# Decoder block with latent attention: the five constant products among the first 22 score chunks are taken out

## The reference, cut to what matters

```python
def mla_attention(x, Wq, Wdkv, Wuk, Wuv, Wo, ln_g, ln_b):
    q = (x @ Wq.T).reshape(b, t, N_HEADS, HEAD_DIM).transpose(0, 2, 1, 3)      # 16 heads of 16
    latent = layernorm(x @ Wdkv.T, ln_g, ln_b)
    k = (latent @ Wuk.T)...; v = (latent @ Wuv.T)...
    q = apply_rope(q); k = apply_rope(k)
    scores = jnp.einsum('bhqd,bhkd->bhqk', q, k) / np.sqrt(HEAD_DIM)
    scores = jnp.where(causal, scores, -jnp.inf)
    attn = jax.nn.softmax(scores, axis=-1)
    out = jnp.einsum('bhqk,bhkd->bhqd', attn, v)...
    return out @ Wo.T
```

## Time and profile before

| what | value |
|---|---|
| median of three runs | 2792.73 us |
| profiled execution | 2797.18 us, span 2795.4 us |
| TensorE busy | 2654.7 us, 95% of the span |
| VectorE, ScalarE, GpSimd busy | 50%, 39%, 11% |
| mean granted TensorE clock | 0.984 |
| DMA | 20 GB/s over the span |

### The profile page before, as it was taken

The page is one execution under the profiler, slowest core; times in us unless marked ns, Lnnn a source line. Parts: engine busy times, 40 slices in busy tenths (PEclk is TensorE's granted clock), DMA queues, the critical chain, the costliest instruction groups (busy, mean ns, idle before and its releaser), DMA issues.

```text
span 2795.4 us, 43692 instructions
## 1 busy us (share of the span) xinstructions
PE 2654.7 (95%) x16702; PEld 1644.3 (59%) x16703; DVE 1395.2 (50%) x3906; ACT 1089.9 (39%) x2028; POOL 299.3 (11%) x457
## 2 busy tenths in 40 slices
PE   7999999999999999999999999999999999978998
PEld 4555655455565664455556564455556564448997
DVE  3334356754334456754333467753343567753443
ACT  3444233543444224444443333434443424431221
POOL 2000010112000010212000010212000010222111
PEclk9999999999999999999999999999999999988999
DMA  3000000001000000001000000001000000032111
GB/s 99 12 12 1 16 1 1 2 14 42 12 12 0 16 1 1 2 14 42 17 7 1 16 1 1 2 14 48 12 6 1 16 1 2 1 149 78 54 56 36
DMA packets 32426, 57.11 MB, mean 20 GB/s; under 512 B 6980, under 2 KB 23442, under 8 KB 31858
## 3 DMA queue, kind: packets, MB, share of 16 engines
q1 hardware_dynamic: 27490, 41.56, 4.7%
q0 software_dynamic: 4752, 13.02, 1.3%
HBM read 40.24 MB, written 14.32 MB: 20 GB/s over the span
## 4 chain that ended last, share of the span: by engine, by line
PE 89%; ACT 4%; DVE 3%; issue 2%; POOL 2%; DMA 0%; SPq 0%; DVEq 0%; ACTq 0%; POOLq 0%
PE ps L959 10%; PE ps L1176 9%; PE ps L931 8%; PE ps L904 8%; PE ps L1210 7%; PE ps L1228 6%; PE ps L889 5%; PE ps L949 5%; PE ps L1303 5%; PE ps L1317 4%; PE ps L914 4%; PE ps L1051 3%; PE ps L1069 2%; PE ps L844 2%; PE ps L860 2%
## 5 line engine op out<-in xcount | busy, mean ns | idle before, releaser
L1405 DVE TENSOR_REDUCE neg_max<-ps 128x1 f32<-128x128 f32 (+7 forms) x256 | 194.1, 758 | 565.6 <-PE ps L934 565.3
L1176 PE MATMUL ps<-arena 32*128 32x512 f32 (+3 forms) x1536 | 446.3, 529 | 11.0 <-DVE arena L1592 6.5
L797 ACT ACTIVATE arena<-ps 128x1024 f32<-128x1024 f32 (+1 forms) x320 | 300.1, 939 | 367.6 <-PE ps L1210 367.5
L1210 PE MATMUL ps<-arena 32*128 32x256 f32 (+1 forms) x2560 | 364.6, 388 | 0.0
L959 PE MATMUL ps<-arena 128*128 128x512 f32 (+3 forms) x768 | 319.6, 503 | 4.7 <-ACT arena L715 0.5
L715 ACT ACTIVATE arena<-ps 128x512 f32<-128x512 f32 (+3 forms) x384 | 188.3, 491 | 296.5 <-PE ps L949 294.4
L931 PE MATMUL ps<-arena 128*128 128x512 f32 (+3 forms) x768 | 290.7, 489 | 4.4 <-ACT arena L724 4.4
L1210 PEld LDWEIGHTS ps<-arena 32*128 32x128 f32 x2560 | 210.5, 183 | 116.3 <-issue 99.3
L904 PE MATMUL ps<-turned_t,arena 128*128 128x512 f32 x512 | 227.8, 598 | 1.1 <-ACT turned_t L686 1.1
L931 PEld LDWEIGHTS ps<-arena 128*128 128x128 f32 x768 | 139.0, 190 | 135.4 <-issue 114.8
L949 PE MATMUL ps<-ident,arena 128*128 128x128 f32 x1152 | 193.1, 278 | 20.8 <-ACT arena L703 11.4
(11 more groups left out here) (215 smaller groups left out, 3852.7 us busy)
## 6 DMA issues: line engine op xcount, KB each, us to landing
arena<-in_w_qkv SPq DMA_DIRECT2D x32, 384.0 KB, 3.1
arena<-in_w SPq DMA_DIRECT2D x2, 4096.0 KB, 16.7
xin<-in_x SPq DMA_DIRECT2D x5, 1024.0 KB, 5.5
xres_ids<-sorted_res SPq DMA_DIRECT2D x35, 129.0 KB, 2.2
xin<-sorted_rows SPq DMA_DIRECT2D x35, 128.0 KB, 2.1
w_out<-in_w_out SPq DMA_DIRECT2D x1, 1024.0 KB
out<-xin,out_row POOLq DMA_INDIRECT x35, 2.8
sorted_res<-xin SPq DMA_DIRECT2D x4, 129.0 KB, 2.5
```

The lines of the kernel that those rows point to most:

```text
L797: nc.scalar.activation(mprobs_t[n % BUFS][:, 2 * pair:2 * pair + 2, 0:QUARTER + more], ps[:, bank:bank + 2, 0:QUARTER + more], ACT.Exp).th ...
L1176: last = nc.tensor.matmul(ps[:, MAX_BANK[m], at:at + n], q_heads_t[rows_j, g, t * P:(t + 1) * P], k_heads_t[rows_j, g, c * BANK:c * BANK + ...
L1210: last = nc.tensor.matmul(ps[:, 3 + j, kb * QUARTER:kb * QUARTER + n_q], k_heads_t[rows_j, g, keys_at:keys_at + P], q_heads_t[rows_j, g, ( ...
L1405: nc.vector.tensor_reduce(neg_max[:, par, t:t + 1], ps[:, buf:buf + 2, :].rearrange("p a n -> p (a n)")[:, 0:n], AX.X, ALU.max, negate=Tru ...
```

## The change

The loop over chunks 6 to 21 with its five calls of `keep_warm` is replaced by one call of `chunks`, which issues the same chunks in the same order. Nothing else is touched: the calls of `keep_warm` at other places stay.

```diff
                 for use in range(NG, 2 * NG):
                     turn_keys(use)
                 pe.wait_ge(kt_taken, b * (2 * NG) + 2 * NG)
-                for s in range(6, ISSUED):
-                    chunks(s, s + 1)
-                    if s % 3 == 2:
-                        keep_warm(1, 7)
+                chunks(6, ISSUED)
                 pe.wait_ge(ms_taken, b * MAX_SLOTS + WIDE)
```

## The result

The changed kernel takes 2819.64 us (median of four runs, 2815.16 to 2820.55) against 2792.72 us before: the ratio of the means is 1.0089, with a 95% interval of 1.0072 to 1.0107. It is slower, by 27 us in the medians, where 11 us were forecast; 2819.64 us also lies above the forecast's own range of 2796 to 2818 us. The profiled execution of it took 2815.16 us with a span of 2813.4 us, 18.0 us more than the profiled execution before. It is the fastest of the four runs, so the profile shows less loss than the median has.

The account below looks back on a forecast made before the run. TensorE, busy for 95% of the span, was taken as the bound. Per batch, 4.7 us lost in items less 1.9 us gained gives +2.8; 2792.7 + 4 x 2.8 = 2803.9, stated as 2804 us (own range 2796 to 2818; 8 in 10: 2788 to 2820).

Parts of the forecast that it names:

- The clock falls in all four batches: Chunks 6 to 21: without constant products, 32-row chunks are too little work, so the clock falls to 0.50 about midway.
- The items: Items after the chunks: 14 us of low clock at 1.5 times the time, 4.7 us lost per batch.
- The chunks: Chunks 6 to 21: low clock costs the last five chunks 1.6 us, leaving 1.9 of 3.5 us gained per batch.
- The sum against the profiled execution: Whole kernel: batches two to four +8.4 us, first batch -1.1, from the profiled 2797.2 us to 2804.5 us.
- The high-clock schedule: Chunk 6 to the items, clock high: chunks 7 to 10 side by side, then VectorE paces; items 3.5 us earlier per batch.
- hold (2779 us): Rival, chunks 6 to 21: the clock holds, each batch keeps its 3.5 us, 2779 us; chance 0.10.
- come back as the items begin (2790 us): Rival, start of items: they restore the fallen clock at once, -0.7 us per batch, 2790 us; chance 0.18.
- stay low through the stage: Rival, items: the clock stays low for a whole stage, 54 to 77 us per batch, 2850 us and above; chance 0.05.

Follow-up runs that it names:

- e1_thin: Changed kernel with the five constant products back at their old places, all 128 rows but 16 columns wide instead of 512: 2827.79 us.
- e3_at_items: Changed kernel plus four full constant products in a row behind chunk 21, before the first item: 2812.44 us, ratio to before 1.0048.
- e9_changed: The changed kernel once more, unaltered, one execution for a second profile: 2824.76 us.
- e5_three: Changed kernel plus three full constant products, after chunks 10, 13 and 16: 2813.72 us, ratio to before 1.0063.
- e2_places: Changed kernel plus four full constant products, after chunks 10, 13, 16 and 19, where TensorE waits: 2788.56 us, ratio to before 0.9954.
- e8_early: Kernel before without the last three of its five constant products, those after chunks 8 and 11 kept: 2817.99 us, one execution.

## Why the prediction was right in its way and wrong in its size

**The clock falls in all four batches**: right, and shown: e1_thin keeps the arrangement and loses the clock, e3_at_items gives the clock back to the items and their time with it. The reason given, that chunks of 32 rows are too little work for the clock, is shown in part: the full products' work is what holds it, but that the number of rows is what counts no run isolates.

**The items.** Forecast: 14 us of low clock in them at 1.5 times the time, 4.7 us lost per batch. Measured in the first profile, from the first score to the end of the fall: 17.6, 15.0, 13.4 and 15.0 us, with losses of 6.2, 5.3, 4.6 and 5.3 us against 21.72. For the second batch 15.0 / (15.0 - 5.3) = 1.55. Both factors were nearly right; in sum the term was 18.8 us and is 21.4.

**The chunks.** This is the step that failed: "For the last five chunks this costs 5 x 0.33 = 1.6 us, so that 1.9 us of the 3.5 are left when the items begin." I let the clock fall "about midway through these chunks". In three batches it fell 3.5 to 5.1 us after chunk 6, with some ten chunks still to be made at the low level, and the items began 15.6 to 15.8 us after chunk 6, later than the 15.24 of before. Only in the first batch, where it fell at 7.6 us, was something left (13.88). Against high-clock passes, 15.25 us each, the chunks' term is 0.0 us over the four batches where -7.6 was forecast. The number of chunks at the low level was wrong: eleven in the second batch, chunks 11 to 21, not five. The extra cost of one was nearly right: against the forecast's high-clock schedule of 11.7 us the second batch loses 4.0 us, 0.37 us per chunk where 0.33 was taken. The 0.94 us per chunk behind that figure are not seen: chunks 11 to 14 take 1068.92 to 1073.48, 1.14 us each.

**The sum against the profiled execution.** Forecast +7.3 us; measured 18.0: 7.6 more from the chunks, 2.6 more from the items, 0.5 from the rest.

**From there to the median.** The median of the changed kernel lies 4.5 us above its profile, and the forecast has no term for such a difference. e9_changed, 2824.76 us, shows what it can consist of. Its span is 9.6 us above that of the first profile: 1.5 us are in the stretches, with one batch of 45.4 us, 4.5 between the last products and the routing's counts (126.0 us in sum), and 2.6 before the first batch's chunk 6, where it has a fall of 6.8 us in the self-attention and the first profile has none. So the difference of the medians, 26.9 us, holds the 21.5 us of four passes with a fall against four without, and some 5 us for which no run near the median was profiled. How often a fall begins early or late I had no row for, and I gave it no term.

**The high-clock schedule** (items 3.5 us earlier per batch) was never run with the clock held, since no run without products held it, so its 3.5 us are not shown. Chunks 7 to 10 do run side by side, and e5_three's 12.50 and e2_places' 12.94 us from chunk 6 to the items, with products, leave room for the schedule's 11.7 with none.

**The rivals.** The clock does not hold (2779 us) and does not come back as the items begin (2790 us): in the two profiles of the changed kernel and in e8_early it is at 0.50 at the first item in all twelve batches. Nor does it stay low through the stage: the longest fall in any of these runs is 37.5 us.

By what the page "TensorE: Matmul & The Clock Gate" of the Trainium skill, section HAM oscillation — how this bites in real kernels, says of long idle gaps, no fall would have come here. In the changed kernel's second batch TensorE has a record for 2.73 of the 3.50 us before the fall and for 11.24 of the 12.30 behind it, and in e1_thin for 3.40 of the 3.40 us before it. To keep idle gaps short was not enough in this stage.

The page "TensorEngine Tiling (Array Packing)" of the Trainium skill, section PSUM Bottleneck, says that tiling speeds up TensorE but not the evacuation of PSUM. The changed kernel's trace agrees: chunks 7 to 10 run side by side in 1.14 us, and VectorE then takes full chunks one by one, 0.61 us apart (1069.39 and 1070.00), while TensorE waits 0.76 us for it.

## What to carry to other kernels

A product that computes nothing can be worth several times its cost where the work around it is narrow: here a product of 1.06 us, five times per batch, kept off falls that cost 5 to 8 us each, as long as there was enough of it all along the narrow stretch. Before removing or thinning such work, read the granted clock of the stretch and of what comes behind it, since the loss falls on the next stage. And put it where the engine waits anyway: four products in TensorE's waits held the clock better than five at regular places (no run above 2791.3 us in nine, where the kernel before has 14 of 30 above 2797), and the stretch before the items took 2.3 us less.

## What the hardware showed that I had not expected

With TensorE's records filling 23.34 of 23.90 us the clock stayed at 0.50 (changed kernel, first batch), on chunks and on the first items. The same items ran at 1.00 throughout in the kernel before, with records in 21.04 of 21.72 us: work that went on at the high level there did not bring the clock back for 13 to 18 us here. So in this stage a busy line in the profile says nothing about the clock. Two passes that are alike to 0.01 us up to the first item can part there, 21.74 against 29.55 us (e5_three), and such a stretch goes with a wide scatter: 25 us over 30 runs of the kernel before, 5.3 us over nine of e2_places.
